# One chunk of the mixture moved behind the maxima, two key products ahead of the last second half, and a copy of the heads' outputs ahead of the root

## The reference

```
q, k, v = x @ Wq.T, x @ Wk.T, x @ Wv.T          # 32 heads of 8; rope on q and k
gate    = q . mean of k over each chunk of 32 keys
allowed = the 4 best chunks of the past and the own chunk, causal
o = softmax(q k / sqrt(8), masked) @ v
o = o * rsqrt(mean(o*o) + 1e-6) * o_norm_weight * sigmoid(x @ Wg1.T @ Wg2.T)
x = layernorm(x + o @ Wo.T)
# mixture of experts: 2 shared and 16 routed experts, 176 hidden units each
s = sigmoid(x @ centroids.T) + bias ; keep the 4 best, normalise to gates
y = x + sum shared relu(x w1 + b1) w2 + b2 + sum gate_e * (relu(x w1_e + b1_e) w2_e + b2_e)
x = layernorm(x + y)
```

## Time and profile before

| | us |
|---|---|
| median of 3 runs | 1563.23 (1561.64 to 5019.03) |
| the profiled execution | 1564.33 |
| its span, first to last instruction | 1562.6 |
| PE busy | 1387.1 (89%) |
| DVE busy | 1180.3 (76%) |
| ACT busy | 846.1 (54%) |
| POOL busy | 539.8 (35%) |
| mean granted TensorE clock | 0.932 of full speed |

### The profile page before, as it was taken

One profiled execution on the slowest core, in us unless ns is written; L12 is line 12 of the kernel. 1 busy time (PEld: TensorE's weight loads), 2 busy tenths in 40 slices (PEclk: granted clock), 3 DMA queues, 4 the chain that ended last, 5 costly groups with the idle time before them and its releaser, 6 DMA issues.

```text
span 1562.6 us, 29670 instructions
## 1 busy us (share of the span) xinstructions
PE 1387.1 (89%) x11024; PEld 755.2 (48%) x11024; DVE 1180.3 (76%) x3027; ACT 846.1 (54%) x1266; POOL 539.8 (35%) x638
## 2 busy tenths in 40 slices
PE   5588899898998989989999899989899899999697
PEld 3322575435643466434654257544664346542364
DVE  7994778867786778967788777876789677885634
ACT  5408663385725765276642957348562776428221
POOL 4204432254323542244422543235322443224143
PEclk8758899998999989999999989999899999998799
DMA  6000021100221012111221002210112101220031
GB/s 239 8 15 8 28 76 64 39 29 29 76 68 35 15 56 75 48 29 29 69 68 43 19 24 82 68 30 28 49 62 68 29 15 61 71 48 15 14 103 60
DMA packets 52212, 77.83 MB, mean 50 GB/s; under 512 B 6322, under 2 KB 26724, under 8 KB 51812
## 3 DMA queue, kind: packets, MB, share of 16 engines
q1 hardware_dynamic: 52068, 75.94, 16.4%
HBM read 67.00 MB, written 8.65 MB: 48 GB/s over the span
## 4 chain that ended last, share of the span: by engine, by line
PE 52%; DVE 19%; issue 10%; ACT 9%; POOL 5%; DVEq 3%; DMA 1%; POOLq 1%; SPq 0%
PE PS L564 12%; PE PS L552 10%; PE PS L704 7%; POOL hp L1029 5%; PE PS L481 4%; DVE CM L1314 4%; ACT UQ L973 3%; PE PS L498 3%; ACT hp L834 3%; DVE hr L1125 2%; PE PS L714 2%; PE PS L760 2%; ACT UK L973 2%; PE PS L401 2%; PE PS L451 2%
## 5 line engine op out<-in xcount | busy, mean ns | idle before, releaser
L1029 POOL TENSOR_TENSOR hp<-hr,hp 128x512 f16<-128x512 f32 (+1 forms) x200 | 234.8, 1174 | 637.0 <-ACT hp L834 605.1
L1314 DVE TENSOR_REDUCE CM<-PS 128x32 f32<-128x1024 f32 x320 | 382.1, 1220 | 47.6 <-PE PS L481 45.1
L564 PE MATMUL PS<-W,hp 128*128 128x256 f16 (+1 forms) x2400 | 322.2, 278 | 26.5 <-POOL hp L1029 23.9
L552 PE MATMUL PS<-x1T,W 128*128 128x512 f16 (+1 forms) x1200 | 315.1, 390 | 0.0
L564 PEld LDWEIGHTS PS<-W,hp 128*128 128x128 f16 (+1 forms) x2400 | 216.4, 99 | 124.4 <-POOL hp L1029 65.0
L825 ACT ACTIVATE hr<-PS,CF 128x512 f32<-128x512 f32 (+1 forms) x200 | 137.3, 686 | 207.4 <-PE PS L552 195.8
L834 ACT ACTIVATE hp<-hr 128x512 f16<-128x512 f32 (+1 forms) x178 | 112.5, 632 | 227.7 <-DVE hr L1125 226.0
L1125 DVE TENSOR_TENSOR hr<-hr,gB 128x512 f32<-128x512 f32 x176 | 121.1, 688 | 84.5 <-ACT hr L825 81.2
L973 ACT ACTIVATE UK<-PS 128x1024 f32<-128x1024 f32 x160 | 152.8, 1036 | 29.0 <-PE PS L498 28.0
L552 PEld LDWEIGHTS PS<-x1T,W 128*128 128x128 f16 (+1 forms) x1200 | 108.8, 101 | 114.9 <-issue 39.7
L973 ACT ACTIVATE UQ<-PS 128x1024 f32<-128x1024 f32 x160 | 151.8, 1044 | 5.2 <-PE PS L498 3.4
(11 more groups left out here) (151 smaller groups left out, 1959.4 us busy)
## 6 DMA issues: line engine op xcount, KB each, us to landing
gB<-gates SPq DMA_DIRECT2D x64, 256.0 KB, 3.2
gB<-gates SPq DMA_DIRECT2D x32, 224.0 KB, 2.8
gB<-gates SPq DMA_DIRECT2D x32, 192.0 KB, 2.8
gB<-gates SPq DMA_DIRECT2D x32, 160.0 KB, 2.5
xT<-in_xT SPq DMA_DIRECT2D x8, 512.0 KB, 3.7
qET<-rows SPq DMA_DIRECT2D x16, 256.0 KB, 5.8
v<-in_x SPq DMA_DIRECT2D x8, 512.0 KB, 4.1
gB<-gates SPq DMA_DIRECT2D x32, 128.0 KB, 2.8
```

Of the source, the lines that this page charges most:

```text
L552: mm = pe.matmul(PS[0:w, BK_H[c % 2], :], W1[:, a, k, bass.ds(f0, w)], x1T[:, e, k, :], start=(n == 0), stop=(n == 5))
L564: mm = pe.matmul(PS[:, BK_Y + j // 2, (j % 2) * D:(j % 2 + 1) * D], hp[0:w, slot, a, j * P:(j + 1) * P], W2[0:w, e, bass.ds(c, 1), :].rear ...
L1029: nc.gpsimd.tensor_tensor(hp[0:w, slot, 1, :], hr[0:w, slot, :], hp[0:w, slot, 0, :], ALU.subtract).then_inc(pool_hp, 1)
L1314: nc.vector.tensor_reduce(dst, src, AX.X, ALU.max).then_inc(dve_cm, 1)
```

## The change

The last stage of the maxima gives one chunk away: chunks 11 to 21 lie beside the maxima, 22 to 24 behind them. `MAX_STEPS` becomes 1, so that the eleven chunks' 77 portions are dealt over all 40 blocks (before, 42 portions over each of two times 20). Behind the maxima PE does `up` of 22 and 23, `down` of 21, the gate products, the turns of tiles 0 and 1, `up` of 24, the turns of tiles 2 and 3, `down` of 22 and 23, then waits for the bias rows, makes key products 0 and 1 of group 0, does `down` of 24, and makes the other key products. ACT does `relu` 22 and 23, `high` 22 and 23, `relu` 24, both `maxima`, the first `output_gate`, `high` 24 and the second `output_gate`. DVE does `gated` of 22, 23 and 24 behind tiles 1, 2 and 3 (before, 23 and 24 behind tiles 1 and 3). In `two_groups`, `copy_outputs(2i + 2)` moves ahead of L1357, the guess and the first Newton step.

```diff
--- before.py
+++ after.py
@@ -64,8 +64,8 @@
 PAIRS = ((0, 1, 0, 1, 0), (2, 1, 0, 2, 1), (0, 1, 2, 0, 1), (2, 0, 1, 2, 1))
 BACK = ((2, 2, 2, 2, 2), (3, 3, 3, 3, 3), (3, 2, 4, 3, 3), (3, 3, 3, 3, 2))

-C_FIRST, C_TOPK, C_MAX, C_BIAS = (0, 3), (3, 11), (11, 23), (23, 25)
-MAX_STEPS = 2
+C_FIRST, C_TOPK, C_MAX, C_BIAS = (0, 3), (3, 11), (11, 22), (22, 25)
+MAX_STEPS = 1
 MU = TU // MAX_STEPS
 MC = (C_MAX[1] - C_MAX[0]) // MAX_STEPS

@@ -652,13 +652,18 @@
                                 down(m, c - 1, (C_MAX[0] + cc - 1) % 2, part - 3)
                             if i == 0 and part == 2 and cc in (1, 2):
                                 selection_rows(c, cc - 1)
-                if m is not None:
+                def late_up(c):
                     for part in range(3):
-                        up(m, NC - 2, part)
-                    for part in range(3):
-                        up(m, NC - 1, part)
+                        up(m, c, part)
+
+                def late_down(c):
                     for j in range(NT):
-                        down(m, NC - 3, (NC - 3) % 2, j)
+                        down(m, c, c % 2, j)
+
+                if m is not None:
+                    late_up(NC - 3)
+                    late_up(NC - 2)
+                    late_down(NC - 4)

                 pe.wait_ge(dve_cm, (b + 1) * TU + RING)
                 for j in (0, 2, 1, 3):
@@ -669,18 +674,16 @@
                         mm.then_inc(pe_g, 1)

                 for j in range(NT):
+                    if m is not None and j == 2:
+                        late_up(NC - 1)
                     pe.wait_ge(dve_bias, b * NT + j + 1)
                     mm = pe.transpose(PS[0:H, 2 + j // 3, j * P:(j + 1) * P], negm[:, j, :], ident)
                     if j >= 2:
                         mm.then_inc(pe_neg, 1)

-                def late_down(c):
-                    for j in range(NT):
-                        down(m, c, c % 2, j)
-
-                if m is not None:
+                if m is not None:
+                    late_down(NC - 3)
                     late_down(NC - 2)
-                    late_down(NC - 1)

                 pe.wait_ge(s_rows, 64 * (b + 1))
                 pe.wait_ge(act_eg, 2 * b + 2)
@@ -725,7 +728,11 @@
                         if t + 3 < NU:
                             unit(g, gs, t + 3)

-                for d in range(NU):
+                for d in range(2):
+                    unit(0, 0, d)
+                if m is not None:
+                    late_down(NC - 1)
+                for d in range(2, NU):
                     unit(0, 0, d)
                 group(1, 1)
                 for i in range(NG // 2 - 1):
@@ -945,12 +952,14 @@
                     nc.scalar.activation(negT[:, s0:s1], PS[0:H, 2 + n, s0:s1], ACT.Copy, scale=1.0 / UNIT).then_inc(act_neg, 1)

                 if m is not None:
-                    relu(m, NC - 2, NC % 2)
+                    relu(m, NC - 3, (NC - 3) % 2)
+                    relu(m, NC - 2, (NC - 2) % 2)
+                    high(m, NC - 3, (NC - 3) % 2)
+                    high(m, NC - 2, (NC - 2) % 2)
                     relu(m, NC - 1, (NC - 1) % 2)
-                    high(m, NC - 2, NC % 2)
                 maxima(0)
+                maxima(1)
                 output_gate(0)
-                maxima(1)
                 if m is not None:
                     high(m, NC - 1, (NC - 1) % 2)
                 output_gate(1)
@@ -1324,8 +1333,8 @@
                                                         in1=CM[:, :, MOFF[j] // CHUNK:MOFF[j] // CHUNK + w],
                                                         op0=ALU.mult, op1=ALU.add))
                     link(nc.vector.tensor_reduce(negm[:, j, :], rep[:, :, 0:w], AX.X, ALU.max, negate=True).then_inc(dve_bias, 1))
-                    if m is not None and j % 2:
-                        gated(m, C_BIAS[0] + j // 2, (C_BIAS[0] + j // 2) % 2)
+                    if m is not None and j >= 1:
+                        gated(m, C_BIAS[0] + j - 1, (C_BIAS[0] + j - 1) % 2)
                 if m is not None:
                     finish(m)
                 def copy_outputs(g):
@@ -1354,12 +1363,12 @@
                     nc.vector.tensor_tensor(sq, u8, u8, ALU.mult)
                     link(nc.vector.tensor_tensor(tok(rt), s1, s1, ALU.mult))
                     link(nc.vector.tensor_reduce(tok(ms), sq, AX.X, ALU.add))
+                    if not last:
+                        copy_outputs(i * 2 + 2)
                     link(nc.vector.scalar_tensor_tensor(out=tok(ms), in0=tok(rt), scalar=HD * 1e-6, in1=tok(ms),
                                                         op0=ALU.mult, op1=ALU.add))
                     root_guess(NT * 2 * HG)
                     newton(NT * 2 * HG, 1)
-                    if not last:
-                        copy_outputs(i * 2 + 2)
                     newton(NT * 2 * HG, 2)
                     link(nc.vector.scalar_tensor_tensor(out=sq, in0=u8, scalar=0.5 * HD ** 0.5,
                                                         in1=tok(ry).unsqueeze(3).to_broadcast([P, NT, 2 * HG, HD]),
```

More of the change, by code:

```diff
@@ L654, in turn @@
                                 selection_rows(c, cc - 1)
-                if m is not None:
-                    for part in range(3):
-                        up(m, NC - 2, part)
-                    for part in range(3):
-                        up(m, NC - 1, part)
-                    for j in range(NT):
-                        down(m, NC - 3, (NC - 3) % 2, j)
+                def late_up(c):
+                    for part in range(3):
+                        up(m, c, part)
+                def late_down(c):
+                    for j in range(NT):
+                        down(m, c, c % 2, j)
+                if m is not None:
+                    late_up(NC - 3)
+                    late_up(NC - 2)
+                    late_down(NC - 4)
                 pe.wait_ge(dve_cm, (b + 1) * TU + RING)
```

## The result

The changed kernel takes 1583.68 us in the median of four runs (1581.76 to 1588.06), the kernel before 1562.43: ratio 1.0132, interval 1.0114 to 1.0149. It is slower by 1.3%; the forecast was 1581. One of the four executions of the kernel before took 5019 us and is left out of the ratio. The profiled execution has a span of 1582.0 us, against 1562.6.

The account below looks back on a forecast made before the run. A DVE-PE loop was taken to bound the maxima, ACT's exponentials the heads. Seven turns of -3.5 + 1.0 + 4.4 and one of +4.4 gave +17.7 us, so 1581 us in the median; range 1553 to 1605.

Parts of the forecast that it names:

- Term 1: Maxima: DVE's nine waits for PE become five, 6.4 us become 3.5, one gate product leaves; 3.5 us less a turn.
- Term 2: Bias and start of heads: first key product starts earlier, but late layernorm delays the first copy; 1.0 us more a turn.
- my list of signs: Expected in the profile after: five waits in the maxima, a 57.5 us stage, mixture's sums 1.5 us behind first key product.
- Term 3: Heads: DVE waits 1.66 us at the moved copy on a closed DVE-PE loop; 4.4 us more in each of eight turns.
- The copies cost nothing: Heads: DVE reaches the copy's new place no earlier than the outputs, so only the other changes count; 1546 us, chance 0.17.
- the nine waits stay: Maxima: PE's own products set the pace, so the stage gains only 0.6 us; 1602 us, chance 0.12.
- nothing to see: Whole kernel: gains and losses cancel, or the copy does what it did; 1563 us, chance 0.09.
- The masks: Heads: each of three pairs loses 1 us more among POOL's masks; 24 us more, 1605 us, chance 0.12.

Follow-up runs that it names:

- the early gate products: The kernel before, with each gate product in the maxima one reduction earlier: 1534.7 us, ratio 0.9820.
- the copy alone: The kernel before with only copy_outputs(2i + 2) moved ahead of L1357: 1603.6 us, ratio 1.0254.
- the fastest kernel: The changed kernel without the moved copy, gate products in the maxima one reduction earlier, first copy inside the closing layernorm: 1511.9 us, ratio 0.9673.
- the last one: The fastest kernel with copy_outputs(2i + 2) moved ahead of L1357 again: 1550.0 us, ratio 0.9912 against the kernel before.

## Why the prediction was right, and where only by cancelling

**Term 1** was right in mechanism and count: five waits, 3.5 us. The stage gained 3.86 us (60.05 to 56.19) where I had 3.5; the early gate products confirm the path. The 57.5 us that I named for the stage were counted from a window of 61.0 us, about 1 us wider than the stage.

**Term 2** came to +1.04 us, forecast +1.0 (22.30 to 23.34 from the maxima's end to the first copy). That it fits so well is luck, for its parts were less exact. I had the wait inside tile 3's addition disappear; it did (0.68 us instead of 1.25), but the new gate product ran into the subtraction instead: it took 1.19 us from 671.15 on, where others take 0.68, and the subtraction (L1038) ran from 670.64 to 671.80. So the last bias came 0.67 us later and not 0.1 to 0.2. The Trainium skill (SBUF — State Buffer, "SBUF: two separate sides") states that a VectorE operation with two SBUF inputs and a GpSimd operation that reads SBUF hold a shared port pair one at a time; the trace agrees, the wait changes its owner but stays. The first key product so gained about 0.1 us here, not 0.45. The sums came 1.9 us later behind the maxima than before, where I had 1.5. (The "1.5 us behind" the first key product in my list of signs doesn't follow from my own times, 676.45 and 678.5, which give 2.05; measured 2.06.) In the turn that I read, the term is 1.79 and not 1.0. Against it, in the kernel before the first copies of two turns stood 2.0 to 2.2 us for PE, a loss that the one turn I read didn't show, and this brings the average down to 1.04.

**Term 3** was the step that carried the forecast, and its loop is the one in the trace: 1.73 us of waiting for 1.66, and 40 us for the copy alone. Its size came out by two errors against each other. First to last copy grew by 6.3 us a turn where I had 5.0 (4.5 for the waits and 0.5 for the masks). At full clock 5.0 is what it costs: the turn from 1249.66, the only one of the changed kernel in which every stretch ran at full clock, takes 37.3 us, and the turn that I read before, also at full clock, 32.4. The masks are in this, though not as I shared them out. The first two loops grew by 1.88 us instead of 1.43, for the DVE path from even to odd copy takes 6.77 us and not 6.3: the moved instructions and the scaling behind them now lie among POOL's masks (L1373 took 0.75 us, the same operation in the kernel before, L1364 at 708.92, 0.43). The third grew by 1.29 instead of 1.67.

What I had not thought of is the clock: eight slow stretches behind odd copies, 12 us in all, and 4.2 us at first copies, of which some 3 come back in shorter DVE paths behind them, make about 1.7 us a turn. The kernel before has no such stretch. It has some 0.5 us a turn of stretches that are long at full clock, which don't come back in the changed kernel; its longest, 6.15 us from 883.85, has a granted clock of 1.00, and in it several small DVE operations are stretched to 0.5 or 0.6 us.

At the turn's end, I had 0.6 us absorbed, and 1.7 were. In the turn that I read, `keep` no longer waited 1.6 but 0.75 us for PE, and the sum of squares, which had taken 0.86 us beside a POOL operation (L1354 at 721.82), took 0.49 (L1363). Net 4.6 a turn for 4.4. The copy alone cost 40 us where eight turns of term 3 make 35.

**The rivals.** "The copies cost nothing" fell with the copy alone, "the nine waits stay" with the five that are left, "nothing to see" with the interval. "The masks" fell too: the extra is 0.45 us in the first two pairs and not 1.

## What to carry to other kernels

Moving a copy forward in an in-order queue pays only up to the moment at which its data are there: read where the producer ends, and put it there, not ahead. Where a wait sits on a loop between two engines, each us of it counts in every round, even if the engines look idle for part of the time (in the changed kernel's heads DVE was busy for 23.2 of 39.5 us and PE for 34.4). Between a producer and its consumer on a long chain through four engines, count the distance in steps of the pacing engine: one step more was worth 29 us here, more than moving a whole chunk of work (10 us alone, 21 in the fastest kernel).

## What the runs showed that I had not expected

PE's clock turns a short wait into a longer one. Each of three kernels, the changed one, the copy alone and the last one, has 16 stretches behind copies 3 and 5, and 8, 9 and 8 of them were slow. In front of every slow one PE had stood 2.0 to 2.5 us for the odd copy; the stretch then lay for part of its time at half clock and took 1.5 us more. A wait of that length did not always do it: the changed kernel has twelve, and four were followed by full clock. Behind its four shorter ones, of 1.49 us, no stretch was slow. None was slow either in the kernel before, where PE stood 0.5 us at most, where the copy was half as far ahead, or where PE had products to do in the wait. The Trainium skill (TensorE: Matmul & The Clock Gate, "HAM oscillation — how this bites in real kernels") describes a PE that falls back to the lower clock behind waits on DMA; here the wait is for another engine's copy.
